# Batch 0's image tokens embedded alone, and a new order of a batch's steps

## Chip, cores and metric

The kernel runs on one core of a Trainium2 chip. The metric is device microseconds of one execution, as the median of several runs; lower is better.

## What is computed

All of it is float32. B = 8 sequences of L = 548 tokens of width D = 192: 36 image tokens, embedded from patches of 768 values, and 512 text tokens given as they are. Then one attention block (3 heads of 64, scores multiplied by a decay matrix before the softmax, a group norm over tokens and channels of each head) and one block of 16 experts, 8 of them weighted per token.

```python
h = concat([patches @ tok_w.T + tok_b, txt], axis=1)                  # (8, 548, 192)
x = layernorm(h)
q, k, v = x @ Wq.T, x @ Wk.T, x @ Wv.T                                # 3 heads of 64
s = (q @ k.T) / 8 * decay          # decay[l, m] = gamma_h ** (m - l) for m >= l, else 0
o = softmax(s) @ v
o = (o - mean) / sqrt(var + eps)   # mean and variance of a head over its tokens and channels
h = h + (o * gn_weight + gn_bias) @ Wo.T
x = layernorm(h)
p = softmax(x @ router_w.T); comb = the 8 largest of p, divided by their sum
h = h + sum over e of comb[:, e] * (gelu(x @ w1[e]) @ w2[e])          # widths 8 x 128, 8 x 256
```

## The kernel before

Five engines run their own instruction streams and meet at semaphores. The order on each engine is written out by hand; there is no planner. A product of float32 numbers is made of several passes over operands split into a rounded part (`_hi`) and a rest (`_lo`): ScalarE writes the rounded part (`copy`, L595), VectorE the rest (`sub`, L945).

**The prologue.** SP issues all loads in one queue (L310 to L321): `gammas`, the patches and the embedding weights in two halves each (`ld_pat`), the bias, the text of batch 0 (`ld_h0`), all attention weights in one transfer (`ld_aw`), the text of batches 1 to 7 (`ld_h`), a share of `w1`, `gn_w`, `gn_b`. Behind them in the same queue it stores the decay rows that VectorE has built (`decay_built`), waits until they have landed and loads them back shifted (`ld_decay`, L323 to L327). TensorE embeds the image tokens of all eight batches at once, 288 columns (L1279 to L1286); ScalarE adds the bias (`emb`, L601, L602), TensorE transposes them in sixteen products (L1291, L1292), VectorE copies them into `h` (`image_tokens`, L920). Before that VectorE has made `drow`, the powers of gamma by doubling (L882), and `aw_lo`, the rest of all attention weights (L890). Then the first layer norm and `x_transpose(0)`.

**A batch.** `body(b, tail, later, more, ahead)` exists once for each engine and is called for b = 0 to 7; `tail` is b > 0, `later` b > 1, `more` b < 7, `ahead` b < 6. In it the third head of batch b-1 is finished while batch b begins, and the output projection of batch b-2 is made inside batch b. TensorE's order is: `qk(b)` (three tiles: q01, q2 and k2, k01), third head's `probs_transpose(b-1, 2)`, `scores_pair(b)`, `attend(b-1, 2)`, `scores_third(b)`, `values(b)`, `project(b-2)`, `probs_transpose(b, 0)`, `attend(b, 0)`, `probs_transpose(b, 1)`, `x_transpose(b+1)`, `attend(b, 1)`, `gn_sums(b-1)`. VectorE's is: `qk_rest(b)` (four rests), `gn_stats(b-1, 0)`, `norm_stats(b+2)` (statistics of a layer norm two batches ahead), `apply_decay` of heads 0 and 1 (L982, with the negated maximum at L989), `normalise(b, 0)` (divides by the softmax's sum, L1006), `apply_decay(b, 2)`, `add_attention(b-2)` and `normalise(b, 1)`, `gn_partial(b-1)`, `x_ext(b+1)` (L954, sums that stand for the masked keys), `x_lo(b+1)`, `gn_variance(b-1)`, `normalise(b, 2)`. Of the third head, `normalise` does three of five tiles; ScalarE scales the other two in the next body:

```python
            def scale_probs(b):
                a.wait_ge(den_ready, nth(b, 1, 1))
                for I in range(2):
                    t = pr[0][:, OFF[I]:OFF[I] + WIDTH[I]]
                    last = a.activation(t, t, ACT.Copy, scale=inv_den[0][:, I:I + 1])
                last.then_inc(probs_scaled, 1)
```

ScalarE also rounds q and k (`qk_round`), makes the exponentials (`exps`, L674), copies transposed probabilities (`pt_copy`) and outputs (`o_copy`; the third head's output goes to both halves of the partitions, four copies), and rounds x (`x_hi`). GpSimd normalises the next batch (`norm_next`), takes the power -0.5 of variances (`rstd_of`, L454), splits a share of `w1` (`halve_w1`, L498 and L501, after `probs_ready` of the first head) and applies the group norm (`gn_coefficients`, `y_values`).

The eight banks of TensorE's accumulator are assigned to the steps by the tuples at L98 to L112; a step waits until what stood in its bank has been read.

**Batch 7 and the hand-over.** In batch 7 the first 512 tokens also get their second layer norm (`second_norm`), transposes (`x2_transpose`), `logits`, the routing (`router_shift`, `router_top`, `router_left`, `router_weights`) and `comb_transpose`; ScalarE copies the result to `ct`, SP stores it and loads it back as `gate`, one row spread over all partitions. The expert part is a loop over nine tiles of tokens and 24 steps (`up`, `gelu`, `weigh` with the gate, L1177, `act_round`, `act_rest`, `down`). In its first tile `beside_first(k)` finishes batch 7's third head and the projections of batches 6 and 7. The residual rows travel through `h_dram` (`store_h`).

Of the kernel before, what the change touches and what calls it, by code (L numbers as in the profile page):

```python
# [32 lines left out]
P = 128  # L33
B = 8
# [70 lines left out]
GN_BANK = 0  # L105
TILE_ORDER = (0, 1, 4, 2, 3)

LAST_PT1 = (1, 3, 0, 6)
LAST_PT2 = (4, 5, 4, 5)
LAST_WO = {5: (2, 7, 6), 6: (4, 5, 2), 7: (4, 5, 2)}  # L110
LAST_GN = {6: 5, 7: 3}
LAST_O = 2  # L112

ATTEND_TILES = ((0, 3, 4), (1, 2))
# [18 lines left out]
def early_fusion(nc, patches, txt, tok_w, tok_b, gammas, gn_w, gn_b, attn_w, w1, w2, out):  # L133
# [9 lines left out]
    with ctx:  # L143
# [102 lines left out]
        ld_aw, ld_pat, ld_gam, ld_gn = sem("ld_aw"), [sem("ld_pat0"), sem("ld_pat1")], sem("ld_gam"), sem("ld_gn")  # L246
# [12 lines left out]
        exp_done, den_ready, probs_ready = sem("exp_done"), sem("den_ready"), sem("probs_ready")  # L259
        probs_scaled = sem("probs_scaled")  # L260
# [40 lines left out]
        def _(sp):  # L301
# [54 lines left out]
            def body(b, tail, later, more, ahead):  # L356
# [11 lines left out]
                if later and more:  # L368
                    store_h(b - 2)
# [25 lines left out]
            store_h(LB - 2)  # L395
# [32 lines left out]
        def _(pool):  # L428
# [57 lines left out]
            def halve_w1(b):  # L486
# [33 lines left out]
            def y_values(t):  # L520
# [5 lines left out]
                for i in range(2):  # L526
                    pool.tensor_scalar(o[:, i, :], o[:, i, :], gscale[:, i:i + 1], gshift[:, i:i + 1], ALU.mult, ALU.add)
                pool.drain()
                for i, dst in enumerate((y01_hi, y2)):
                    pool.tensor_copy(dst[:, :], o[:, i, :]).then_inc(y_hi, 1)  # L530
                pool.drain()
                for i, (p0, lo, hi) in enumerate(((0, y01_lo, y01_hi), (HD, y2, y2))):
                    if i:
                        pool.drain()
                    pool.tensor_tensor(lo[p0:P, :], o[p0:P, i, :], hi[p0:P, :], ALU.subtract).then_inc(y_lo, 1)
# [21 lines left out]
            def body(b, tail, later, more, ahead):  # L557
# [33 lines left out]
        def _(sc_eng):  # L591
# [6 lines left out]
            a.wait_ge(ld_aw, 16)  # L598
            copy(aw_hi[:, :, :], aw_raw[:, :, :]).then_inc(aw_hi_ready, 1)
            a.wait_ge(emb_done, 1)  # L600
            a.activation(emb[:, 0, :], ps[:, 0, 0:B * IMG], ACT.Identity, bias=tokb[:, 0:1])  # L601
            a.activation(emb[0:HD, 1, :], ps[0:HD, 1, 0:B * IMG], ACT.Identity, bias=tokb[0:HD, 1:2]).then_inc(emb_copied, 1)  # L602

            def round_router():

                a.wait_ge(aw_lo_ready, 1)
# [30 lines left out]
            def scale_probs(b):  # L637

                a.wait_ge(den_ready, nth(b, 1, 1))
                for I in range(2):  # L640
                    t = pr[0][:, OFF[I]:OFF[I] + WIDTH[I]]
                    last = a.activation(t, t, ACT.Copy, scale=inv_den[0][:, I:I + 1])  # L642
# [1037 lines left out]
```

## Time and profile before

| | |
|---|---|
| median of 3 runs | 796.58 us (795.94 to 799.67) |
| profiled execution, its own time | 794.4 us |
| its span, first to last instruction | 792.1 us |
| TensorE busy, matmuls | 744.4 us (94%), 4400 instructions |
| VectorE busy | 551.0 us (70%) |
| ScalarE busy | 485.9 us (61%) |
| GpSimd busy | 155.8 us (20%) |
| transfers | 60.74 MB, mean 77 GB/s |

The span of the profile is what an order of instructions can change; the execution's own time lies 2.3 us above it. PE is TensorE, PEld its weight loads, DVE VectorE, ACT ScalarE, POOL GpSimd, SPq the queue from which SP issues transfers. A name such as L945 is a line of the kernel, often that of a helper: `sub` and `copy` serve many steps. "issue" is idle time for which the profile shows no wait.

### The profile page before, as it was taken

How to read it: one execution, taken by the hardware profiler on the slowest of the kernel's cores; microseconds unless marked ns; L12 is line 12 of the kernel's file. 1: busy time of each engine (PE TensorE's matmuls, PEld its weight loads, DVE VectorE, ACT ScalarE, POOL GpSimd, SP SyncE). 2: the span in 40 equal slices, each digit the busy share in tenths (PEclk: the TensorE clock that was granted, in tenths of full speed). 3: DMA queues.
4: the chain of work that ended last, by engine and by line, in shares of the span. 5: the costliest groups of instructions: out<-in, count | busy, mean ns of one | idle time of the engine just before them, and what ended most of it. 6: DMA issues, size and time to landing. Idle time of an engine off the chain costs nothing.

```text
span 792.1 us, 13238 instructions
## 1 busy us (share of the span) xinstructions
PE 744.4 (94%) x4400; PEld 635.0 (80%) x4400; DVE 551.0 (70%) x1548; ACT 485.9 (61%) x1087; POOL 155.8 (20%) x261
## 2 busy tenths in 40 slices
PE   6688898999988999999999999999999999999997
PEld 2577787888886777788888888888888888888885
DVE  5588888889788676576567566576666666665654
ACT  1368897897886846456556456556465564564443
POOL 2034436535542780010010010010000100100000
PEclk9689999999998999999999999999999999999999
DMA  7500010011031462242242241342241332412410
GB/s 223 167 2 21 21 42 22 23 42 43 2 100 41 121 184 60 77 127 72 58 115 69 77 128 39 86 125 55 78 120 52 86 104 62 109 62 70 113 50 19
DMA packets 44390, 60.74 MB, mean 77 GB/s; under 512 B 4018, under 2 KB 37762, under 8 KB 44322
## 3 DMA queue, kind: packets, MB, share of 16 engines
q1 hardware_dynamic: 44322, 59.91, 26.5%
q8 instruction: 34, 0.56, 0.3%
q14 instruction: 34, 0.28, 0.1%
HBM read 51.84 MB, written 8.05 MB: 76 GB/s over the span
## 4 chain that ended last, share of the span: by engine, by line
PE 71%; ACT 12%; DVE 7%; issue 4%; POOL 3%; DVEq 1%; POOLq 1%; DMA 0%; SPq 0%
PE ps L1271 67%; ACT pt L595 3%; ACT pr L674 3%; DVE sc L982 2%; ACT ot L595 2%; ACT pr L642 1%; ACT k_hi L595 1%; DVE pr L1006 1%; PE ps L1400 1%; POOL w_lo L553 1%; PE ps L1451 1%; DVE nm L989 1%; ACT xa_hi L595 1%; DVE k_lo L945 1%; POOLq L552 1%
## 5 line engine op out<-in xcount | busy, mean ns | idle before, releaser
L1177 DVE TENSOR_TENSOR act<-act,gate 128x480 f32<-128x480 f32 (+1 forms) x216 | 144.8, 671 | 115.8 <-ACT act L788 110.7
L1271 PE MATMUL ps<-x,w_hi 128*128 128x480 f32 (+1 forms) x648 | 217.0, 389 | 0.2 <-ACT act L788 0.2
L788 ACT ACTIVATE act<-ps 128x480 f32<-128x480 f32 (+1 forms) x216 | 123.7, 573 | 130.2 <-PE ps L1271 130.1
L1271 PE MATMUL ps<-x,w_lo 128*128 128x480 f32 (+1 forms) x432 | 165.9, 384 | 0.0
L945 DVE TENSOR_TENSOR act_lo<-act,act_hi 128x480 fp32r<-128x480 f32 (+1 forms) x216 | 145.0, 671 | 0.2
L1271 PEld LDWEIGHTS ps<-x,w_hi 128*128 128x128 f32 x648 | 121.6, 188 | 21.2 <-ACT act L788 0.7
L595 ACT ACTIVATE act_hi<-act 128x480 fp32r<-128x480 f32 (+1 forms) x216 | 130.7, 605 | 6.8 <-DVE act L1177 6.7
L1271 PEld LDWEIGHTS ps<-x,w_lo 128*128 128x128 f32 x432 | 81.2, 188 | 13.4
L1271 PE MATMUL ps<-act_hi,w_hi 128*128 128x480 f32 (+1 forms) x216 | 83.5, 387 | 4.5 <-DVE act_lo L945 4.5
L1271 PE MATMUL ps<-act_hi,w_lo 128*128 128x480 f32 (+1 forms) x216 | 82.5, 382 | 0.0
L1271 PE MATMUL ps<-act_lo,w_hi 128*128 128x480 f32 (+1 forms) x216 | 82.5, 382 | 0.0
L454 POOL TENSOR_TENSOR rstdb<-vepsb,neg_half 128x4 f32<-128x4 f32 x9 | 11.7, 1303 | 359.2 <-DVE vepsb L1069 359.2
L1271 PE MATMUL ps<-act_lo,w_r 128*128 128x480 f32 (+1 forms) x216 | 82.4, 381 | 0.0
L1271 PE MATMUL ps<-act_hi,w_r 128*128 128x480 f32 (+1 forms) x216 | 82.2, 381 | 0.0
L674 ACT ACTIVATE pr<-sc,nm 128x580 f32<-128x580 f32 (+4 forms) x120 | 66.4, 557 | 17.2 <-DVE nm L989 17.1
L1400 PE MATMUL ps<-ident,pr 128*128 128x128 f32 (+1 forms) x360 | 44.5, 274 | 16.9 <-ACT pr L642 6.9
L1400 PEld LDWEIGHTS ps<-ident,pr 128*128 128x128 f32 (+1 forms) x360 | 38.5, 132 | 22.0 <-issue 11.3
L595 ACT ACTIVATE pt<-ps 128x384 f32<-128x384 f32 (+3 forms) x120 | 46.2, 472 | 13.8 <-PE ps L1400 13.6
L982 DVE CUSTOM_DVE_ANT_0 sc<-ps,decay 128x548 f32<-128x548 f32 (+4 forms) x120 | 49.3, 453 | 4.7 <-PE ps L1271 4.5
L1271 PEld LDWEIGHTS ps<-act_hi,w_hi 128*128 128x128 f32 x216 | 40.4, 187 | 14.5 <-DVE act_lo L945 6.8
L1271 PEld LDWEIGHTS ps<-act_hi,w_r 128*128 128x128 f32 x216 | 40.5, 188 | 7.1
L1271 PEld LDWEIGHTS ps<-act_lo,w_r 128*128 128x128 f32 x216 | 40.5, 188 | 7.0
(181 smaller groups left out, 1257.0 us busy)
## 6 DMA issues: line engine op xcount, KB each, us to landing
gate<-comb_dram SPq DMA_DIRECT2D x112, 240.0 KB, 3.2
gate<-comb_dram SPq DMA_DIRECT2D x32, 256.0 KB, 3.8
w_raw<-w SPq DMA_DIRECT2D x16, 384.0 KB, 3.7
h_dram<-h SPq DMA_DIRECT2D x8, 384.0 KB
res<-h_dram SPq DMA_DIRECT2D x7, 360.0 KB, 4.4
out<-res SPq DMA_DIRECT2D x7, 360.0 KB, 3.2
h<-txt SPq DMA_DIRECT2D x3, 672.0 KB
decay_rows<-drow SPq DMA_DIRECT2D x1, 1014.0 KB, 8.4
```

The lines of the kernel that those rows point to most:

```text
L454: pool.tensor_tensor(rs[:, :], ve[:, :], neg_half[:, 0:n], ALU.pow)
L552: pool.drain()
L553: pool.tensor_tensor(w2_lo[:, part, :], raw[:, :, 0:P], w2_hi[:, part, :], ALU.subtract)
L595: return a.activation(dst, src, ACT.Copy)
L642: last = a.activation(t, t, ACT.Copy, scale=inv_den[0][:, I:I + 1])
L674: last = a.activation(pr[s][:r, cols], sc[s][:r, cols], ACT.Exp, bias=nm[s][:r, I:I + 1], accum_out=row_sum[s][:r, I:I + 1])
L788: a.activation(act[j % 3][:, 0:n], ps[:, up_bank(j), 0:n], ACT.Gelu_apprx_tanh).then_inc(gelu_done, 1)
L945: return dve.tensor_tensor(dst, src, hi, ALU.subtract)
L982: dve.tensor_tensor_reduce(out=sc[s][:r, OFF[I]:OFF[I] + n], in0=psf[:r, at:at + n], in1=decay[:r, hh, 0:n], scale=1.0 / 8, scalar=0.0 if ...
L1177: dve.tensor_tensor(act[j % 3][:, 0:n], act[j % 3][:, 0:n], gate[e % 4][:, 0:n], ALU.mult).then_inc(gated, 1)
L1271: return pe.matmul(dst, w, x, start=start, stop=stop)
L1400: return pe.transpose(ps[:n, bank, at:at + P], pr[s][:, src:src + n], ident[:, :])
```

## The change

It has four parts.

1. **Prologue.** The patches come as two inputs, batch 0's (36 columns) and the rest (252). SP loads batch 0's first, the rest only behind batch 0's text and the first part of the attention weights; the attention weights come in two transfers (q and k; all others). TensorE embeds batch 0 alone; the first 128 channels of the rest follow before `x_transpose(0)`, the last 64 inside batch 0 between the two heads' scores and the third's, and their transposes around `values(0)`. ScalarE's and VectorE's shares move likewise (`embedded`, `image_tokens(1)` to `(4)`, `weights_hi(i)`, `weights_lo(i)`). The powers of gamma are made in three portions with other steps between.
2. **Third head.** `scale_probs` is gone, and `normalise(b, 2)` scales all five tiles on VectorE. The third head's output is copied once (two copies), and `y2`, the group norm's statistics and values use 64 partitions for it.
3. **Order in a batch.** `qk` makes q01, k01, then q2 and k2; `scores_pair` waits for the first two tiles' rests alone. `o_copy(b-1, 1)` moves into the next body. `probs_transpose(b-1, 2)` waits for the first `q_lo` with all its groups. On VectorE, `norm_stats(b+2)` moves from before the first decay to after `add_attention(b-2)`, which is whole and after `normalise(b, 1)`. On GpSimd `halve_w1` goes ahead of `rstd_of(b+2)`. The banks are assigned anew.
4. **Batch 7.** `project(5)` and `add_attention(5)` stand where they do in other batches, `store_h(5)` is issued in SP's body, `x2_transpose` and `logits` move behind `attend(7, 0)`, and `up(0)`, `comb_transpose(0)`, `up(1)` end the batch. Small steps of `beside_first` change places.

The core of the diff:

```diff
-X_BANKS = (6, 1)
-QK_BANKS = (4, 6, 1)
-SCORE_BANKS = [(2, 4), (0, 5), (2, 6)]
-V_BANKS = ((4, NT - 1, 1), (0, 0, 2), (1, 2, 2))
-PT_BANKS = [(1, 3, 2, 6), (1, 3, 0, 4), (0, 3, 4, 5)]
-O_BANKS = (5, 3, 7)
-WO_BANKS = (5, 4, 0)
+X_BANKS = (1, 6)
+QK_BANKS = (4, 1, 6)
+SCORE_BANKS = [(0, 7), (3, 2), (0, 6)]
+V_BANKS = ((7, NT - 1, 1), (3, 0, 2), (4, 2, 2))
+PT_BANKS = [(4, 1, 0, 6), (6, 0, 3, 5), (3, 4, 5, 2)]
+O_BANKS = (4, 0, 5)
+WO_BANKS = (2, 3, 7)
...
 # SP
+            sp.dma_start(pat[:, :, 0:IMG], first_patches).then_inc(ld_pat[0], 16)
             for i in range(2):
                 part = slice(i * KT // 2, (i + 1) * KT // 2)
-                sp.dma_start(pat[:, part, :], patches[:, part, :]).then_inc(ld_pat[i], 16)
                 sp.dma_start(tokw[:, part, :], tok_w[:, part, :]).then_inc(ld_pat[i], 16)
             sp.dma_start(tokb[:, :], tok_b).then_inc(ld_pat[1], 16)
             load_h(0, 1, ld_h0)
-            sp.dma_start(aw_raw[:, :, :], attn_w).then_inc(ld_aw, 16)
+            sp.dma_start(aw_raw[:, :, 0:QK_W], attn_w[:, :, 0:QK_W]).then_inc(ld_aw[0], 16)
+            sp.dma_start(pat[:, :, IMG:B * IMG], patches).then_inc(ld_pat[2], 16)
+            sp.dma_start(aw_raw[:, :, QK_W:AW], attn_w[:, :, QK_W:AW]).then_inc(ld_aw[1], 16)
             load_h(1, B, ld_h)
...
 # GpSimd, body
+                halve_w1(b)
                 if ahead:
                     pool.drain()
                     rstd_of(b + 2, ln1_var, rstd, mv, veps, nmr, ln1_rstd)
-                halve_w1(b)
...
 # ScalarE, body
                 qk_round(b, 1)
                 if tail:
-                    scale_probs(t)
-                for part in (2, 3):
-                    qk_round(b, part)
+                    o_copy(t, 1, O_BANKS[1])
+                qk_round(b, 2)
+                qk_round(b, 3)
...
 # VectorE, normalise
-                for I in range(2 if hh == 2 else 0, NT):
+                for I in range(NT):
...
 # VectorE, body
                 qk_rest(b)
                 if tail:
                     gn_stats(t, 0)
-                if tail and ahead:
-                    dve.wait_ge(ln1_rstd, nth(b, 1, 2))
-                    norm_stats(b + 2, st6, mv, veps, ln1_var)
...
                 apply_decay(b, 0)
                 apply_decay(b, 1)
+                normalise(b, 0)
                 if not tail:
+                    dve.wait_ge(ld_h, 16 * NT)
+                    image_tokens(1)
+                    image_tokens(2)
+                    dve.drain()
                     norm_stats(1, st6, mv, veps, ln1_var)
-                normalise(b, 0)
                 apply_decay(b, 2)
-                if later and more:
-                    add_attention(b - 2, WO_BANKS, (0,))
...
+                normalise(b, 1)
+                if not tail:
+                    image_tokens(3)
+                    image_tokens(4)
+                    dve.drain()
+                if later:
+                    add_attention(b - 2, WO_BANKS)
+                if ahead:
+                    dve.wait_ge(ln1_rstd, nth(b, 1, 2))
+                    norm_stats(b + 2, st6, mv, veps, ln1_var)
...
 # TensorE
+            embed(0, 0, 0, IMG)
+            embed(1, 1, 0, IMG).then_inc(emb_done, 1)
             pe.wait_ge(emb_copied, 1)
             pe.wait_ge(consts, 2)
+            image_transpose(0)
+            pe.wait_ge(ld_pat[2], 16)
+            embed(0, 0, IMG, B * IMG).then_inc(emb_done, 1)
...
-                    probs_transpose(t, 2, (0,))
-                    pe.wait_ge(o_copied, nth(t, 3, 2))
                     pe.wait_ge(qk_lo, nth(b, 4, 1))
-                    probs_transpose(t, 2, (1, 2, 3))
+                    probs_transpose(t, 2, (0, 1, 2))
+                    pe.wait_ge(qk_lo, nth(b, 4, 2))
+                    probs_transpose(t, 2, (3,))
                 scores_pair(b, tail)
                 if tail:
                     attend(t, 2, O_BANKS[2])
+                else:
+                    embed(1, IMG_REST, IMG, B * IMG).then_inc(emb_done, 1)
                 scores_third(b)
...
                 attend(b, 0, O_BANKS[0])
+                if not more:
+                    pe.wait_ge(wo_added, nth(b - 2, 3, 3))
+                    x2_transpose(0, 1, LAST_X2[1])
...
+                if not more:
+                    up(0)
+                    comb_transpose(0, LAST_X2[1])
+                    up(1)
```

## Rows read from the trace of the kernel before

**Rows 1.** Busy time by stage: start:end, length, each engine's busy time (instructions).

```profile
0.00:29.10 29.10, 16.21 (x51) 7.29 (x51) 17.60 (x74) 5.75 (x8) 6.04 (x26) 0.88 0.76 234
...
29.10:300.00 270.90, 243.08 (x2007) 214.03 (x2008) 221.98 (x785) 210.85 (x581) 131.92 (x207) 0.96 0.18 54
```

**Rows 2.** Busy time by batch, the same columns, from one `x_ext` to the next.

```profile
112.66:140.88 28.22, 26.12 (x241) 23.63 (x240) 24.69 (x93) 23.83 (x69) 14.29 (x23) 1.00 0.10 30
...
197.36:225.37 28.01, 25.92 (x241) 23.61 (x240) 22.80 (x82) 23.93 (x69) 12.74 (x20) 1.00 0.09 31
```

**Rows 3.** Timeline, TensorE, batch 3: start, length, what, idle time before.

```profile
120.17 1.80 PE L1400 MATMUL ps<-ident,pr 128*68 128x128 f32 x15 [0.98 <-ACT pr L642]
...
122.41 0.50 PE L1271 MATMUL ps<-k_hi,q_hi 64*128 64x512 f32 x2 [0.44 <-ACT pt L595]
...
124.19 0.41 PE L1271 MATMUL ps<-k_hi,q_hi 64*128 64x292 f32 x2
```

**Rows 4.** Timeline, ScalarE, batch 3.

```profile
113.56 0.65 ACT L595 ACTIVATE xa_hi<-ps 128x580 fp32r<-128x580 f32 x1
...
118.70 1.33 ACT L642 ACTIVATE pr<-pr,inv_den 128x580 f32<-128x580 f32 x2
```

**Rows 5.** Timeline, VectorE, batch 3.

```profile
112.66 1.30 DVE L954 TENSOR_REDUCE ps<-ps 128x4 f32<-128x512 f32 x2
...
116.86 0.17 DVE L996 TENSOR_TENSOR den<-zero_score,lower_count 128x5 f32<-128x5 f32 x1
...
117.62 0.80 DVE L1006 TENSOR_SCALAR pr<-pr,inv_den 128x324 f32<-128x324 f32 x3
...
118.34 0.72 DVE L945 TENSOR_TENSOR q_lo<-ps,q_hi 128x548 fp32r<-128x548 f32 x1
...
122.81 1.37 DVE L900 BATCH_NORM_STATS2 st<-h 128x6 f32<-128x192 f32 x5
...
124.96 0.73 DVE L982 CUSTOM_DVE_ANT_0 sc<-ps,decay 128x548 f32<-128x548 f32 x1
...
130.71 1.58 DVE L1006 TENSOR_SCALAR pr<-pr,inv_den 128x580 f32<-128x580 f32 x5
...
132.21 0.71 DVE L982 CUSTOM_DVE_ANT_0 sc<-ps,decay 128x548 f32<-128x548 f32 x1
...
134.54 1.00 DVE L989 TENSOR_SCALAR nm<-mx 128x4 f32<-128x4 f32 x1
...
139.23 0.79 DVE L1012 BATCH_NORM_STATS2 gst<-ot 128x6 f32<-128x274 f32 x2
```

**Rows 6.** Timeline, GpSimd, batch 3.

```profile
133.54 1.97 POOL L501 TENSOR_TENSOR w_lo<-w_raw,w_hi 128x384 fp32r<-128x384 f32 x2
```

**Rows 7.** Timeline, prologue and batch 0: TensorE's first product, VectorE.

```profile
5.68 10.71 PE L1271 MATMUL ps<-pat,tokw 128*128 128x288 f32 x24 [5.68 <-DMA tokw<-tok_w]
...
22.45 1.47 DVE L920 COPY h<-ps 36x384 f32<-36x384 f32 x3
...
40.55 0.73 DVE L982 CUSTOM_DVE_ANT_0 sc<-ps,decay 128x548 f32<-128x548 f32 x1 [2.81 <-PE ps L1271]
```

**Rows 8.** SP's queue; transfers of the first 60 us: size, us to landing; queue's share.

```profile
23.26 0.55 SPq L324 DMA_DIRECT2D decay_rows<-drow  x1
...
decay_rows<-drow SPq DMA_DIRECT2D x1, 1014.0 KB, 8.4
...
decay<-decay_rows SPq DMA_DIRECT2D x1, 822.0 KB, 4.3
...
q1 hardware_dynamic: 6592, 7.70, 41.1%
```

**Rows 9.** Batch 7 to the first `weigh`: busy time, ScalarE's `ct`, VectorE.

```profile
225.37:268.24 42.87, 37.28 (x295) 32.13 (x294) 33.23 (x131) 34.29 (x95) 19.03 (x33) 0.92 0.24 70
...
261.32 0.59 ACT L595 ACTIVATE ct<-ps 16x512 f32<-16x512 f32 x1 [0.87 <-PE ps L1470]
...
268.24 1.29 DVE L1177 TENSOR_TENSOR act<-act,gate 128x512 f32<-128x512 f32 x2 [0.17 <-issue]
```

More of the change, by code:

```diff
@@ L130, in nth, with early_fusion @@
     return b * per + k
-def early_fusion(nc, patches, txt, tok_w, tok_b, gammas, gn_w, gn_b, attn_w, w1, w2, out):
+def early_fusion(nc, first_patches, patches, txt, tok_w, tok_b, gammas, gn_w, gn_b, attn_w, w1, w2, out):
     ctx = ExitStack()
@@ L525, in y_values @@
                 o = ot[t % 2]
[L526 to L535, printed above, removed]
+                for i, r in enumerate(Y_ROWS):
+                    pool.drain()
+                    pool.tensor_scalar(o[:r, i, :], o[:r, i, :], gscale[:r, i:i + 1], gshift[:r, i:i + 1], ALU.mult, ALU.add)
+                for i, hi in enumerate((y01_hi, y2)):
+                    pool.drain()
+                    pool.tensor_copy(hi[:Y_ROWS[i], :], o[:Y_ROWS[i], i, :]).then_inc(y_hi, 1)
+                for i, (lo, hi) in enumerate(((y01_lo, y01_hi), (y2[HD:P, :], y2))):
+                    pool.drain()
+                    pool.tensor_tensor(lo, o[:Y_ROWS[i], i, :], hi[:Y_ROWS[i], :], ALU.subtract).then_inc(y_lo, 1)
                 pool.drain()
@@ L635, in two @@
                 return ap.rearrange("p (a n) -> p a n", a=2)
[L637 to L642, printed above, removed]
-                last.then_inc(probs_scaled, 1)
             def qk_round(b, part):
-                dst, p0, i = ((q01_hi[:, :], 0, 0), (q2[0:HD, :], 0, 1), (k2_hi[HD:P, :], HD, 1), (k01_hi[:, :], 0, 2))[part]
+                dst, p0, i = ((q01_hi[:, :], 0, 0), (k01_hi[:, :], 0, 1), (q2[0:HD, :], 0, 2), (k2_hi[HD:P, :], HD, 2))[part]
                 a.wait_ge(qk_done, nth(b, 3, i + 1))
@@ L701, in o_copy @@
                 for half, n in enumerate(ATTEND_W):
-                    for p in ((0,), (HD,), (0, HD))[hh]:
-                        last = copy(ot[b % 2][p:p + HD, hh // 2, at:at + n], ps[HD * half:HD * half + HD, bank, 0:n])
+                    p = HD * (hh % 2)
+                    last = copy(ot[b % 2][p:p + HD, hh // 2, at:at + n], ps[HD * half:HD * half + HD, bank, 0:n])
                     at += n
@@ L756, in body @@
                 v_copy(b, (2,))
-                if not more:
-                    x2_round(0, 0, 5)
-                    x2_round(0, 1, 4)
                 exps(b, 1, (2, 3, 4))
@@ L931, in _ @@
             norm_join(st6, mv, veps, ln1_var)
-            for i in range(1, B // 2):
-                last = image_tokens(i)
-            last.then_inc(embt_copied, 1)
+            decay_powers(256, L - 1).then_inc(decay_built, 1)
             norm_share(0, rstd, nmr, ln1_rstd, xn, first_normed)
+            weights_lo(0)
             for t in (0, 1):
@@ L1164, in body @@
                 normalise(b, 2)
-                if not more:
-                    add_attention(b - 2, LAST_WO[b - 2])
             x_ext(0)
             x_lo(0)
+            weights_lo(1)
             iterations(body)
@@ L1316, in qk @@
                 for i in range(3):
-                    tile, bank = (0, 2, 1)[i], QK_BANKS[i]
+                    tile, bank = i, QK_BANKS[i]
+                    if i == 0 and not tail:
+                        pe.wait_ge(aw_lo_ready, 1)
                     if i == 0 and tail:
                         pe.wait_ge(o_copied, nth(b - 1, 3, 1))
+                        pe.wait_ge(pt_copied, nth(b - 1, 4 * H, 4 * 2))
                     ah, al, bh, bl = weights(tile * P, (tile + 1) * P)
@@ L1545, in down @@
+            x_transpose(0)
+            iterations(body)
             def down(j):
@@ L1661 @@
     arrays = {
[L1662 removed]
+        "first_patches": img.transpose(1, 0, 2)[:, :, 0:IMG],
+        "patches": img.transpose(1, 0, 2)[:, :, IMG:],
         "txt": f(txt),
```

326 lines of the change are left out of this document (174 added, 152 removed).

## The prediction

> **What bounds the kernel now.** I read the page first: TensorE is busy for 744.4 of 792.1 us, so all that an order of work can win lies in 47.7 us of its idle time, and a table by stage shows where. The prologue up to the first projection is 16.2 busy of 29.1 and leaves 12.9; the eight attention batches and the hand-over up to 300 us are 243.1 busy of 270.9 and leave 27.8 [rows 1]; so 7.0 of the 47.7 remain for the expert part's 492 us. The change leaves the expert part as it is after its first tile, so its gain must come from the first 300 us.
>
> One batch then, by the start of `x_ext` (L954) in each. Batches 1 to 6 take 27.4, 28.1, 28.2, 27.8, 28.7 and 28.0 us (batches 3 and 6 stand in [rows 2]), and 2 to 5 have a mean of 28.2, with TensorE busy about 26.1, VectorE 24.7 and ScalarE 23.8. In TensorE's timeline of batch 3 two gaps end on ScalarE: 0.98 us until it has scaled the third head (L642), 0.44 until it has copied `pt` [rows 3]; a third, before the second head's transposes, ends on VectorE. The 2.1 us idle are all that TensorE can be given back: 26.1 us is the floor of a batch. ScalarE's chain leads into the first: its scaling of two tiles takes 1.33 us and stands between the rounding of `q` and of `k` [rows 4]. VectorE has no long wait at all: its 24.7 us busy understate it, since each `drain` and each small operation leaves a little time that is neither busy nor free [rows 5]. That is the view which decides here.
>
> **The change in the steady batches.** Off ScalarE go the 1.33 us of scaling and two of the four copies of the third head's output. Onto VectorE goes the scaling: five tiles take 1.58 us where three take 0.80, so +0.78 [rows 5]. `norm_stats(b+2)`, 2.15 us from 122.81 to 124.96, today lies between `qk_rest` and the first decay, just while TensorE makes the scores VectorE needs. The change puts it behind `add_attention`, ahead of `gn_partial` and of `x_ext(b+1)`. There nothing covers it: behind it wait `x_ext`, then ScalarE's `x_hi`, then TensorE's next projections.
>
> So I add up VectorE's chain from one `x_ext` to the next, in the new order, with today's start-to-start times [rows 2, 4, 5]:
> - `x_ext` to `x_hi`: 0.65 and a handover, 0.73; both `x_hi` and the four remaining exponentials, 113.56 to 116.86: 3.30. Together 4.03. (VectorE's own `x_lo` and `gn_variance` are done at 3.9, and hide here.)
> - `normalise(b-1, 2)`: 116.86 to 118.34 is 1.48 with three tiles, +0.78 with five: 2.26.
> - `q_lo` of the first tile: 0.75, and 0.1 until TensorE sees it, since the third head's transposes now wait for it.
> - fifteen transposes: 1.80, less a little overlap, 1.73; their copies by ScalarE end as they do.
> - scores of tiles 0, 1 and 4: 122.41 to 124.19 plus the end of the last product, 2.04 [rows 3]. VectorE meanwhile has the other three parts of `qk_rest` and `gn_stats`, 2.9 us, and idles 1.0.
> - both decays and `normalise(b, 0)`, 124.96 to 132.21: 7.25.
> - third decay, `normalise(b, 1)` and `add_attention`, 132.21 to 139.23, less one drain: 6.93.
> - `norm_stats` 2.15 and `gn_partial`, 139.23 to 140.88, where batch 3 ends: 1.65.
>
> The sum is 28.9 us, where a batch now takes 28.2. The scaling leaves ScalarE's chain, but only to lengthen VectorE's, and the statistics lose their cover; TensorE waits for `q_lo` (1.0) and for `x_hi` (1.0) in place of the gaps it loses. TensorE's own chain in the new order ends about 0.9 before it is needed, so it does not decide. Batches 2 to 5: 4 x 0.7 = +2.8. Batch 1 has no `add_attention` (1.44): 27.5 against 27.4, +0.1. Batch 6 has no `norm_stats`: VectorE would need 26.75, TensorE brings `x_transpose` at about 27.0, so 27.0 against 28.0 [rows 2]: -1.0. Sum of the batches: +1.9.
>
> One term can go. In batch 3 a 128x4 negation (L989), elsewhere 0.17 us, takes 1.00 and ends at the same time as a subtraction of GpSimd (L501, 133.54 to 135.51) [rows 5, 6]. Six of the seven batches from 1 to 7 show 1.00, batch 4 shows 0.33. What starts the subtraction, `probs_ready` of the first head, is the same in the new order, so by the rows I keep the 0.85 us. If it went everywhere, a batch would be 28.05 and the sum of the batches -1.5. The Trainium skill has a rule for this (SBUF — State Buffer, section "SBUF: two separate sides"): VectorE in a two-port mode and GpSimd hold a shared pair of ports exclusively for a whole instruction, and the one that starts first makes the other wait. By that rule, the trace agrees, and a start moved by a fraction of a microsecond could turn the order round; that would be the 28.05.
>
> The bounds: a batch of 26.4 (TensorE's floor and a little) below, 29.4 above (0.5 more, should GpSimd's `y_values` also hold up the two new scalings). I take 28.9.
>
> **The prologue.** Today the first products start at 5.68 and take 10.71 us for 288 columns [rows 7]. With 36 columns an eighth of the streaming is left, and the weight loads between set the pace: 6 us, an estimate between an eighth and the whole of 10.7, nearer its middle. Then two transposes instead of sixteen, the copy of `aw_lo` out of VectorE's way, and the first layer norm's power at about 14.7 instead of 22.6: some 8 us earlier, as far as the first projection. The scores gain 1.4 more, since `k01` is now the second tile projected. They would be ready about 9 us earlier, and the decay could start at 32 instead of 40.55.
>
> But the decay matrix is not there. Its store is issued at 23.26, after all loads of SP's queue, and lands 8.4 later; its load follows and takes 4.3: it lands at 36.0 [rows 8]. Today that is hidden by 4.5 us. The store waits not for `decay_built` (about 16 after the change) but behind the loads, whose bytes stay the same. The packets become more: patches 256 to 1,536, attention weights 128 to 512, 1,664 in all. From nothing extra to, at the mean 60 ns of a packet (41.1% of 16 engines for 60 us by 6,592 packets [rows 8]), 6.2 us over 16 engines; since the bytes do not grow I take 0.8. The decay lands at 36.8 and VectorE starts at 36.9: 3.65 earlier than now [rows 7]. From 9 us, 5 are lost to this wait.
>
> Batch 0 then pays for what was moved into it. From the first decay to `x_ext(1)` it takes 16.65 us today (40.55 to 57.20). Added are four copies of image tokens (1.47 for three today [rows 7], so 1.9 with drains), ScalarE's second `emb` copy 0.5, ahead of the exponentials for which `normalise(0, 0)` waits, and 0.4 for the values, which now follow the image transposes: 19.5. `x_ext(1)` comes at 56.4, where it was 57.2: -0.8.
>
> **Batch 7 and the hand-over.** Projecting batch 5 earlier fills a gap of TensorE, but `x2_transpose(0, 1)` now waits for `add_attention(5)` (a bank of its own output), at 27.8 us after `x_ext(7)`; logits, shift, `second_norm(1)`, top and weights follow on VectorE, and `comb` is copied to `ct` at 37.6 after it. Today's copy ends at 261.91, 36.5 after it. The gates load from there: the first `weigh` starts 6.3 us behind it [rows 9]; I take 5.4 of that for the store and the gate, the rest for what VectorE still had to do: 43.0 after `x_ext(7)` against 42.87 now. The order inside is better, the end is set by the same road; VectorE no longer has the late `add_attention`, but waits for a gate instead. I take 0, from -3 (fewer waits in the first expert tile) to +3.5.
>
> **Sum.** -0.8 + 1.9 + 0 = +1.1 on the span of 792.1. That execution took 794.4, the median shown is 796.6, 2.2 above it; carried to the median: 797.6, rounded to 797.5. What this measurement can tell from no change is about 0.5%, 4 us.
>
> **The rivals.**
> 1. The batches fall to TensorE's floor. For it: TensorE is at 26.1 of 28.2 and two of its three gaps end on the removed scaling. Against: the chain above, which has no slack for it. Batches 1 to 6 at 26.4 each would save about 10: 787.
> 2. The decay comes sooner. The transfer engines are busy for 41.1% of the first 60 us [rows 8], so there is room; if the new order fills that, landing at 32 makes the prologue's 8 us real: -4.9 further, 792.
> 3. The other side: TensorE's clock at the hand-over. Batch 7 shows a mean granted clock of 0.92, the batches before it 1.00 [rows 2, 9]: 42.87 x 0.08 x 2, some 6.9 us at 0.5, the 1.2 GHz level. In the new order TensorE has nothing between `up(1)` at about 38 and the first `down` at 45 but two short pieces. If those gaps lower the clock as the first products of the expert part run, 6.8 us at half rate cost 3.4: 801. It decides once the gap before the first `down` exceeds some 2 us and the clock falls behind it and not before.
> 4. Nothing in the prologue is hidden and a batch costs 28.05: 795; inside no change.
>
> **Chances.** Forecast with rival 4: 0.56. Rival 1: 0.13. Rival 2, alone or with the stall gone: 0.12. Rival 3, or a batch of 29.4: 0.19. So faster 0.25, same 0.56, slower 0.19. Rival 1 in full and half of what lies above 801 stay outside: 790.5 to 801.5.
>
> **What the profile after would show.** The first decay starting right after `ld_decay`, near 37, with TensorE idle or embedding before it: right. A start near 32 makes rival 2 true. Batches of 28.5 to 29 with VectorE idle only before the first decay and TensorE waiting for `q_lo` and `xa_hi`: right; 26.5 makes it wrong. `norm_stats` between `add_attention` and `gn_partial` followed at once by `x_ext`: right. `ct` copied 37 to 38 after `x_ext(7)`: right; 34 would bring the end forward by 3.

## The result: half a per cent slower, and the profile after

The changed kernel takes 800.57 us (median of 12 runs, 797.01 to 802.74), the kernel before 796.24 (794.62 to 799.67): ratio 1.0052, 95% interval 1.0039 to 1.0066. That is +4.3 us where I had forecast about +1, inside the range. The two profiled executions stand further apart than the medians, 800.2 against 792.1 us of span, since the execution profiled of the kernel before (794.4) lies 1.8 below its median and that of the kernel after (802.0) 1.4 above. Of their 8.1 us this is the account, each term the difference of two starts in the traces: `x_ext(1)` comes 0.4 earlier (56.79 for 57.20); batches 1 to 6 take 4.6 more; `x_ext(7)` to the first `weigh` 0.3 more; from there to the end 3.6 more.

Busy time by stage of the kernel after (start:end, length, then PE, PEld, DVE, ACT, POOL with instructions, the granted clock, share and GB/s of the transfers), answering to [rows 1, 2, 9]:

```profile
0.00:36.15 36.15, 21.05 (x126) 17.07 (x126) 18.87 (x80) 9.79 (x18) 6.10 (x26) 0.96 0.73 214
36.15:56.79 20.64, 18.55 (x119) 15.12 (x121) 18.30 (x78) 12.80 (x40) 7.58 (x13) 0.73 0.01 2
113.15:142.29 29.14, 26.51 (x239) 23.69 (x239) 25.30 (x96) 21.88 (x64) 14.69 (x23) 1.00 0.10 29
142.29:172.55 30.26, 27.88 (x239) 25.19 (x239) 25.36 (x95) 21.89 (x64) 14.39 (x23) 0.94 0.09 29
201.40:229.60 28.20, 25.69 (x221) 23.73 (x221) 23.45 (x84) 21.50 (x63) 13.04 (x21) 0.94 0.07 23
229.60:272.80 43.20, 35.35 (x299) 30.35 (x297) 34.79 (x137) 31.20 (x88) 19.43 (x33) 1.00 0.25 72
272.80:800.20 527.40, 515.29 (x2486) 436.84 (x2486) 334.91 (x729) 286.31 (x530) 41.81 (x61) 0.99 0.30 85
```

ScalarE has lost 2 us a batch, as the change meant (21.9 where [rows 2] have 23.8), and the batch is longer. VectorE's busy time has grown by 0.6 (25.3 for 24.7), and its timeline has one long wait. VectorE's timeline of batch 3 after, the lines that answer to [rows 5]:

```profile
113.15 1.29 DVE L972 TENSOR_REDUCE ps<-ps 128x4 f32<-128x512 f32 x2
...
117.23 0.17 DVE L1014 TENSOR_TENSOR den<-zero_score,lower_count 128x5 f32<-128x5 f32 x1 [0.20 <-ACT pr L675]
...
118.29 1.58 DVE L1022 TENSOR_SCALAR pr<-pr,inv_den 128x580 f32<-128x580 f32 x5 [0.38 <-issue]
119.80 0.71 DVE L963 TENSOR_TENSOR q_lo<-ps,q_hi 128x548 fp32r<-128x548 f32 x1
...
124.60 0.73 DVE L1000 CUSTOM_DVE_ANT_0 sc<-ps,decay 128x548 f32<-128x548 f32 x1 [1.13 <-PE ps L1286]
...
131.86 0.72 DVE L1000 CUSTOM_DVE_ANT_0 sc<-ps,decay 128x548 f32<-128x548 f32 x1
...
134.19 1.02 DVE L1007 TENSOR_SCALAR nm<-mx 128x4 f32<-128x4 f32 x1
...
138.72 1.39 DVE L917 BATCH_NORM_STATS2 st<-h 128x6 f32<-128x192 f32 x5
...
140.78 0.77 DVE L1028 BATCH_NORM_STATS2 gst<-ot 64x6 f32<-64x274 f32 x2
...
142.29 0.69 DVE L972 TENSOR_REDUCE ps<-ps 128x4 f32<-128x512 f32 x1
```

The one wait on another engine's work of any length is the 1.13 us before the first decay. TensorE's timeline of the same batch shows its two long waits, for `x_hi` and for the first `q_lo`:

```profile
114.68 0.49 PE L1286 MATMUL ps<-xa_hi,aw_hi 128*128 128x274 f32 x2 [1.00 <-ACT xa_hi L597]
...
120.61 1.80 PE L1435 MATMUL ps<-ident,pr 128*68 128x128 f32 x15 [1.11 <-DVE q_lo L963]
122.44 0.50 PE L1286 MATMUL ps<-k_hi,q_hi 64*128 64x512 f32 x2
```

And GpSimd's subtraction, with whose end the negation L1007 ends (135.2):

```profile
133.21 1.98 POOL L504 TENSOR_TENSOR w_lo<-w_raw,w_hi 128x384 fp32r<-128x384 f32 x2
```

The prologue, by SP's queue, in place of [rows 8]: the text of batches 1 to 7 holds the queue for 11.5 us, and the decay matrix comes behind it.

```profile
8.16 11.53 SPq L309 DMA_DIRECT2D h<-txt  x3
...
23.98 0.43 SPq L328 DMA_DIRECT2D decay_rows<-drow  x1
31.60 0.38 SPq L331 DMA_DIRECT2D decay<-decay_rows  x1
```

VectorE's timeline shows what that costs, where [rows 7] had a wait of 2.81 for TensorE:

```profile
25.38 0.73 DVE L963 TENSOR_TENSOR k_lo<-ps,k_hi 64x548 fp32r<-64x548 f32 x1
36.15 0.73 DVE L1000 CUSTOM_DVE_ANT_0 sc<-ps,decay 128x548 f32<-128x548 f32 x1 [10.04 <-DMA decay<-decay_rows]
```

The hand-over in TensorE's timeline: short pieces between waits of 1.6, 2.2 and 2.7 us, and then the first `down` at the lower clock, a product every 0.43 us (277.77, 278.20) where experiment 7 has one every 0.23.

```profile
266.16 0.61 PE L1503 MATMUL ps<-ident,comb 128*16 128x128 f32 x4 [1.64 <-DVE comb L1131]
...
270.18 0.50 PE L1286 MATMUL ps<-x,w_hi 128*128 128x512 f32 x1 [2.24 <-ACT act L799]
...
275.15 1.17 PE L1435 MATMUL ps<-ident,pr 128*128 128x128 f32 x7 [2.67 <-ACT pt L597]
277.18 0.79 PE L1286 MATMUL ps<-act_hi,w_hi 128*128 128x512 f32 x1 [0.86 <-DVE act_lo L963]
277.77 0.63 PE L1286 MATMUL ps<-act_hi,w_lo 128*128 128x512 f32 x1
```

Last, stages cut where the granted clock changes, in batch 4 and at the hand-over:

```profile
142.70:146.10 3.40, 2.13 (x13) 1.67 (x14) 2.99 (x8) 3.09 (x10) 0.00 (x0) 1.00 0.00 0
146.10:149.50 3.40, 3.40 (x17) 3.40 (x17) 2.98 (x11) 1.92 (x6) 2.38 (x6) 0.50 0.01 2
...
270.00:275.80 5.80, 2.95 (x19) 2.42 (x20) 1.40 (x2) 2.19 (x6) 5.23 (x10) 1.00 0.78 230
275.80:282.60 6.80, 5.94 (x18) 3.84 (x17) 3.29 (x5) 2.76 (x6) 5.42 (x8) 0.50 0.53 138
```

At 0.50, 1.2 GHz, TensorE is busy for all of the 3.40 us in batch 4, but starts a projection's product every 0.23 us where 0.13 is usual. Batch 4 with such a stretch takes 30.26 us, its neighbours 29.14 and 28.85; there is another in batch 6 (204.1 to 207.5). The kernel before had none in batches 1 to 6. In all it had as much half-clock time as the changed one, 27.3 us ahead of the last products, but elsewhere: from 22.0 to 35.6, 39.0 to 45.9 and 250.7 to 257.5 (in batch 7), where the changed one has 33.5 to 47.1, the two stretches in batches and 275.8 to 282.6 (behind the first `weigh`).

### The profile page after: what moved, and what is told of

The parts are those of the page before. It is cut to its first block, busy times and chain, and to the rows that moved or that the text cites. A ratio compares the mean times of both kernels' runs of the same rounds, so it can differ in the third digit from the quotient of the medians.

```text
span 800.2 us, 13292 instructions
## 1 busy us (share of the span) xinstructions
PE 747.7 (93%) x4424; PEld 640.7 (80%) x4424; DVE 554.9 (69%) x1568; ACT 471.3 (59%) x1058; POOL 154.6 (19%) x261
## 4 chain that ended last, share of the span: by engine, by line
PE 68%; DVE 16%; ACT 4%; issue 3%; SPq 3%; DVEq 3%; DMA 2%; POOL 0%; POOLq 0%
PE ps L1286 64%; DVE sc L1000 4%; DVE pr L1022 3%; ACT pr L675 2%; DVE nm L1007 2%; SPq L309 2%; PE ps L1435 1%; DMA decay_rows<-drow 1%; PE ps L1484 1%; DVE h L1066 1%; DVE st L917 1%; DVEq L1005 1%; DMA gate<-comb_dram 1%; DVE act L1192 1%; ACT xa_hi L597 1%
## 5 line engine op out<-in xcount | busy, mean ns | idle before, releaser
L597 ACT ACTIVATE pt<-ps 128x384 f32<-128x384 f32 (+3 forms) x120 | 46.2, 470 | 12.1 <-PE ps L1435 11.5
```

The source lines that it names most:

```text
L597: return a.activation(dst, src, ACT.Copy)
```

## The experiments

Each is told as its difference from the changed kernel, unless it says otherwise. Ratios are to the kernel before.

**1. `norm_stats(b+2)` back before the first decay**, in batches 1 to 5.

```diff
                 if tail:
                     gn_stats(t, 0)
+                if tail and ahead:
+                    dve.wait_ge(ln1_rstd, nth(b, 1, 2))
+                    norm_stats(b + 2, st6, mv, veps, ln1_var)
...
-                if ahead:
+                if ahead and not tail:
```

> The changed kernel with one step put back: norm_stats(b+2) of batches 1 to 5 stands on VectorE before the first decay again, all else as changed. Theory (VectorE's chain has lost the cover of these statistics): the 1.0 us in which VectorE waits for the scores is filled, the first decay starts 1.1 us later and x_ext(b+1) comes 1.0 us earlier, so batches 1 to 5 take 27.9 us where they take 28.9, and TensorE's wait for x_hi (1.0 us) shrinks to some 0.1; 5 us less, 795 to 796 us. If the two short stretches of TensorE's lower clock in batches 4 and 6 came from these waits, they go too, and it is 793 to 795. Rival (the banks or the later q_lo set the batch): batches stay at 28.9, 800 us.

Measured: 796.74 us, ratio 0.9993 (0.9980 to 1.0007). Batches 2 to 5 take 28.45, 28.57, 28.26 and 28.27. The move is worth 0.5 us a batch, half of what I expected: 2.4 us of statistics go into a gap of 1.1 and push the first decay back by 1.4. In batch 3, L923, elsewhere 0.17 us, takes 0.61 and ends with a subtraction of GpSimd's `y_values` (124.73 to 126.08). This execution has no stretch at half clock in the batches, which accounts for 2.8 of the 4.9 us by which its profile is shorter than the changed kernel's; the median is 3.8 below.

**2. Scaling of two tiles back on ScalarE**, in `scale_probs` before `o_copy(b-1, 1)`, with its two semaphores.

```diff
-                for I in range(NT):
+                for I in range(2 if hh == 2 else 0, NT):
...
                 if tail:
+                    scale_probs(t)
                     o_copy(t, 1, O_BANKS[1])
```

> The changed kernel with ScalarE scaling two of the third head's five tiles again, between the rounding of k01 and o_copy(b-1, 1). Theory (one chain through both engines): VectorE is free 0.78 us earlier, but ScalarE, which now also has o_copy(b-1, 1) there, starts its copies of pt 1.3 us later, so the scores start at 10.0 us after x_ext in place of 8.9: a batch takes about 1 us more, 29.9, and the kernel 806 us. Rival (the scaling on VectorE is what made the batch long): 0.78 us less in each of six batches, 28.1, and 796 us.

Measured: 807.69 us, ratio 1.0145 (1.0128 to 1.0163). Batches 1 to 6 take 28.6 to 30.3; the first decay comes 12.5 us after `x_ext` where the change has 11.2. The rounding of q2 and k2 stands behind the scaling on ScalarE. This part of the change does pay, in the order around it.

**3. The decay matrix ahead of the text of batches 3 to 7** in SP's queue.

```diff
-            load_h(1, B, ld_h)
+            load_h(1, 3, ld_h)
...
             sp.dma_start(decay[:, :, :], shifted[:, :, 0:L]).then_inc(ld_decay, 16)
+            load_h(3, B, ld_h3)
...
                     dve.wait_ge(ln1_rstd, nth(b, 1, 2))
+                    if b == 1:
+                        dve.wait_ge(ld_h3, 16 * NT)
                     norm_stats(b + 2, st6, mv, veps, ln1_var)
```

> The changed kernel with SP's queue in another order: the text of batches 1 and 2, the share of w1 and gn_w, gn_b, then the decay rows' store and load, and the text of batches 3 to 7 last, with a wait for it before norm_stats(3). Theory (the decay matrix's way through the queue hides what the new prologue gained): the store is issued at about 14 to 16 us, the matrix has landed at 26 to 28 in place of 36.1, the first decay starts there and x_ext(1) comes at 47 to 49 where it comes at 56.8; 8 us less, 792 us. Rival (the transfers themselves are the limit, or the text of batches 1 and 2 comes too late): the first decay starts earlier, but x_ext(1) moves by less than 3 us.

Measured: 790.29 us, ratio 0.9931 (0.9914 to 0.9947): 10.3 below the changed kernel. SP's queue and VectorE's first decay:

```profile
8.38 1.99 SPq L309 DMA_DIRECT2D h<-txt  x3
...
14.08 0.38 SPq L328 DMA_DIRECT2D decay_rows<-drow  x1
22.00 0.38 SPq L331 DMA_DIRECT2D decay<-decay_rows  x1
```

```profile
26.84 0.73 DVE L1001 CUSTOM_DVE_ANT_0 sc<-ps,decay 128x548 f32<-128x548 f32 x1 [1.06 <-PE ps L1289]
```

The decay now waits for TensorE's scores, which are there at 26.8, 13.7 us earlier than in the kernel before. (In the changed kernel itself TensorE makes them from 24.15 to 27.1, and they wait there until 36.15.) So the prologue of the change was worth 13.7 us and all but 4.4 of it stood behind a transfer.

**4. The kernel before with `norm_stats(b+2)` behind `add_attention`**, that step of the change alone.

```diff
-                if tail and ahead:
-                    dve.wait_ge(ln1_rstd, nth(b, 1, 2))
-                    norm_stats(b + 2, st6, mv, veps, ln1_var)
...
+                if ahead:
+                    dve.wait_ge(ln1_rstd, nth(b, 1, 2))
+                    norm_stats(b + 2, st6, mv, veps, ln1_var)
```

> The kernel before with one part of the change alone: norm_stats(b+2) of batches 1 to 5 moves on VectorE from before the first decay to after add_attention(b-2), ahead of gn_partial. Theory (uncovered there): the first decay starts 0.5 us earlier, x_ext(b+1) about 1.6 us later, and with 0.2 us of slack in ScalarE's x_hi a batch takes 1.4 us more, 29.6 in place of 28.2; 7 us more, 803 us. Rival (ScalarE's chain sets the batch there, and VectorE has room): no more than 2 us, 796 to 798.

Measured: 798.71 us, ratio 1.0030 (1.0016 to 1.0044), batches 2 to 5 have a mean of 28.8 (28.2 before): 0.6 longer, not 1.4. VectorE's timeline of its batch 3 (the first decay, and the negation that took 1.00 in [rows 5]):

```profile
125.10 0.73 DVE L982 CUSTOM_DVE_ANT_0 sc<-ps,decay 128x548 f32<-128x548 f32 x1 [1.68 <-PE ps L1267]
...
134.51 0.17 DVE L989 TENSOR_SCALAR nm<-mx 128x4 f32<-128x4 f32 x1
```

The 2.15 us are uncovered, but GpSimd's `halve_w1`, which in the order of before stands behind `rstd_of` and so behind these statistics, starts only at 142.26: the stall of 0.85 goes, and the first decay comes 0.5 earlier. In the changed kernel `halve_w1` was moved ahead of `rstd_of`, and so the stall stayed.

**5. `halve_w1` after the second head's probabilities.**

```diff
-                pool.wait_ge(probs_ready, nth(b, H, 1))
+                pool.wait_ge(probs_ready, nth(b, H, 2))
```

> The changed kernel, in which GpSimd's halve_w1 starts after probs_ready of the second head instead of the first. Theory (VectorE's chain sets the batch, and 0.85 us of it is the negation L1007 that ends with GpSimd's subtraction): the negation falls from 1.02 to 0.17 us, batches 1 to 6 shorten by up to 0.85 each, to a mean of about 28.1 from 28.8; the span falls by 4 to 5 us to about 796. Rival: the subtraction then meets another small VectorE instruction, or delays GpSimd's power for the next statistics, and the batches stay at 28.8: 800.

Measured: 794.20 us, ratio 0.9965 (0.9952 to 0.9978): 6.4 below the changed kernel for one digit. Batches 2 to 5 take 28.00, 28.27, 27.99 and 28.00, and batch 6 26.53. Of the 6.9 us by which batches 1 to 6 are shorter in this profile, 2.8 are the two half-clock stretches, which it lacks, and 4.0 the stalls. VectorE's timeline of batch 5, in which the negation of the third head is back at 0.17:

```profile
180.51 0.73 DVE L1000 CUSTOM_DVE_ANT_0 sc<-ps,decay 128x548 f32<-128x548 f32 x1 [1.20 <-PE ps L1286]
...
190.03 0.17 DVE L1007 TENSOR_SCALAR nm<-mx 128x4 f32<-128x4 f32 x1
```

**6. Products that nobody reads in TensorE's two waits of a batch** (1 to 6); they change no output.

```diff
+                    filler(GN_BANK, 8)     # before the wait for q_lo
...
+                        filler(5, 7)       # after gn_sums
```

> The changed kernel, in which TensorE makes products that nobody reads in its two waits of about 1 us in batches 1 to 6: eight 128x128 transposes while it waits for the first q_lo, seven after gn_sums while it waits for x_hi. Theory (the granted clock of 0.5 at 146 to 150 us and at 204 to 208 us follows from those waits, and it is what makes batches 4 and 6 take 30.3 and 28.2 instead of 28.9 and 27.0): no stretch at 0.5 inside batches 1 to 6, batch 4 near 28.9, batch 6 near 27.5, the span 2 to 3 us less: 797.5. Rival: the falls come from something else (or the added products, some 0.1 us too long, cost as much as they save): batches of 28.9 to 29.2, falls remain somewhere, 800 to 802.

Measured: 798.11 us, ratio 1.0012 (0.9998 to 1.0026), 2.5 below the changed kernel. The profiled execution has no stretch at half clock in batches 1 to 6; batch 4 takes 28.83, batch 6 26.77.

**7. The same at the hand-over**: 12 and 16 products behind `up(0)` and `up(1)`, 18 between the groups of `pt`.

```diff
                     up(0)
+                    filler(2, 12)
                     comb_transpose(0, LAST_X2[1])
                     up(1)
+                    filler(2, 16)
...
                     probs_transpose(LB, 2, (0, 1), LAST_PT2)
+                    filler(2, 18)
```

> The changed kernel, in which TensorE makes 12, 16 and 18 products that nobody reads around comb_transpose and between the groups of pt in the first expert tile. Theory (the granted clock of 0.5 from 275.8 to 282.6 us follows from TensorE's waits of 1.6, 2.2 and 2.7 us before it, and takes about 3.4 us of the first expert tile): that stretch is gone or starts before the first weigh, and the time from the first weigh to the end falls by 3 us: span 797. Rival: the first expert tile is longer because of its order (the last groups of pt behind act_round), and only 0 to 1 us comes back: 800.

Measured: 798.39 us, ratio 1.0024 (1.0006 to 1.0042), 2.2 below the changed kernel. Its stage from the first `weigh` to the end, and the first `down` in TensorE's timeline:

```profile
270.58:794.80 524.22, 514.43 (x2502) 436.67 (x2500) 337.29 (x729) 286.53 (x530) 43.69 (x61) 1.00 0.30 86
```

```profile
274.23 0.50 PE L1286 MATMUL ps<-act_hi,w_hi 128*128 128x512 f32 x1 [0.30 <-DVE act_lo L963]
274.56 0.39 PE L1286 MATMUL ps<-act_hi,w_lo 128*128 128x512 f32 x1
```

524.2 against 527.4: 3.2 us come back, and the kernel before had 523.9. The batches of this kernel are those of the change, yet this execution had no stretch at half clock in them either: batch 4 took 28.83 and batch 6, in the first row here, 26.78. The second row is batch 6 of experiment 3, whose order there is the same, with a stretch (193.5 to 196.9):

```profile
200.65:227.43 26.78, 24.43 (x221) 22.30 (x221) 23.33 (x85) 21.38 (x63) 13.06 (x21) 1.00 0.08 25
```

```profile
190.54:218.78 28.24, 25.73 (x221) 23.81 (x221) 23.41 (x84) 21.50 (x63) 13.08 (x21) 0.94 0.07 23
```

So a stretch inside a batch costs 1.4 us, and whether one comes changes from one execution to the next. That this is part of why 12 runs of the change spread over 5.7 us is likely: those above 801 us have a mean granted clock of 0.981 to 0.984, those below 800 one of 0.984 to 0.988. In the medians the gain of this edit is not clear of the noise: its interval touches that of the change (1.0039 to 1.0066).

**8. Edits 1, 3 and 5 together.**

> The changed kernel with three edits together: norm_stats back before the first decay (alone: -4.9 us in the span), the decay matrix stored and loaded before the text of batches 3 to 7 (alone: -11.3), halve_w1 after the second head. Theory (the three act at different places of VectorE's chain, and add up; with the norm early, L1007's stall is again 0.85 in six batches, and going it leaves batches near 27.5): span 789 - 5 - 3 to 5 = 779 to 781, ratio near 0.98. Rival (TensorE, 26.1 us busy in a batch and waiting for x_hi, becomes the bound, or the clock falls oftener as it waits less evenly): 784 to 787.

Measured: 782.64 us, ratio 0.9824 (0.9799 to 0.9849), span 781.9, just outside what the theory gave, and better than the rival. Batches 4 and 5 take 27.97, no less than with edit 5 alone. VectorE and GpSimd at the end of its batch 4:

```profile
156.94 0.76 DVE L1038 TENSOR_TENSOR gtmp<-gmv 128x2 f32<-128x2 f32 x1
```

```profile
155.72 1.96 POOL L505 TENSOR_TENSOR w_lo<-w_raw,w_hi 128x384 fp32r<-128x384 f32 x2
```

The stall has moved: now a product of 128x2 numbers, elsewhere 0.16 us, waits for the end of the subtraction, at 157.7.

**9. Edits 3 and 5 without edit 1.**

> The changed kernel with the decay matrix ahead of the text of batches 3 to 7 and with halve_w1 after the second head, but norm_stats where the change put it (late). Theory (in the kernel with all three edits the early norm_stats gives nothing, since GpSimd's subtraction then meets VectorE's small subtraction L1038 in gn_partial, 0.76 us in place of 0.16): batches of 28.0 here too, ratio as with three edits, 0.982 within 0.002. Rival (the early norm_stats does give 0.5 us a batch): 785, ratio 0.986.

Measured: 783.53 us, ratio 0.9832 (0.9809 to 0.9855). The early `norm_stats` gives nothing once the other two are in: theory right.

**10. Experiment 8 with the subtraction of `halve_w1` behind the start of `x_ext(b+1)`**, and `rstd_of(b+2)` ahead of `halve_w1`.

```diff
+                if b < LB:
+                    pool.wait_ge(xt_ext, nth(b + 1, 2, 1))
                 for c in range(2):
                     last = pool.tensor_tensor(w1_lo[:, c, cols], w1_raw[:, c, :], w1_hi[:, c, cols], ALU.subtract)
```

> The changed kernel with norm_stats early, the decay matrix early, and halve_w1 in two pieces on GpSimd: the power of rstd_of(b+2) first, the rounding of w1 after the second head, its subtraction (1.96 us) only when x_ext(b+1) has started, where VectorE reads the accumulator. Theory (a small VectorE instruction on the SBUF that meets this subtraction waits for its end, and large ones that read the accumulator don't): L1038 takes 0.16 instead of 0.76, batches 2 to 5 take 27.4 instead of 28.0 to 28.4, the span is 3 us below the 781.9 of the three edits: 779. Rival: the power or the subtraction meets another instruction there (the negations in the decays, or x_lo), and the batches stay at 28.0 or above: 782 or more.

Measured: 783.78 us, ratio 0.9831 (0.9810 to 0.9851); batches 4 and 5 27.95. VectorE's timeline around the start of batch 4:

```profile
129.44 0.16 DVE L1043 TENSOR_TENSOR gtmp<-gmv 128x2 f32<-128x2 f32 x1
...
130.10 1.30 DVE L978 TENSOR_REDUCE ps<-ps 128x4 f32<-128x512 f32 x2 [0.26 <-PE ps L1351]
131.67 0.76 DVE L969 TENSOR_TENSOR xa_lo<-ps,xa_hi 128x580 fp32r<-128x580 f32 x1 [0.27 <-ACT xa_hi L603]
...
142.12 0.71 DVE L929 TENSOR_SCALAR veps<-mv 128x5 f32<-128x5 f32 x1
```

The stall is gone (0.16), and the batch is as long: `x_ext` now waits for TensorE's transposes, and L929, elsewhere 0.17 us, takes 0.71 and ends with a subtraction of `y_values`, so that stall has only changed its place. My theory was right about the stall and wrong about its worth.

**11. The same with the products of experiment 7.**

> As the run before with halve_w1 in two pieces, and with TensorE's added products around comb_transpose and between the groups of pt (12, 16 and 18). Theory (they keep the granted clock at 1.00 through the first expert tile, which gave 3.1 us from the first weigh to the end when they were added alone): 1 to 3 us below that run, 776 to 778. Rival (the clock's falls are elsewhere by now, before the first weigh): within 1 us of it.

Measured: 782.04 us, ratio 0.9813 (0.9790 to 0.9837). From the first `weigh` to the end 524.6 us, and 524.2 without the added products, where the half-clock stretch (253.5 to 256.9) began before the first `weigh` (255.7) and was over before the first `down` (259.3). The rival was right in substance; the batches are 27.96 again, and one (batch 1) has a stretch at half clock. Experiments 8 to 11 can't be told from each other; all are 1.7 to 1.9% faster than the kernel before.

## Why the prediction came out as it did

**The steady batch: right, by its own terms.** 28.9 forecast; batches 2, 3 and 5, which have no half-clock stretch, take 28.83, 29.14 and 28.85. By the lines of batch 3 above: 4.08 until the exponentials are done (4.03 forecast), 2.57 for the denominators and `normalise(b-1, 2)` (2.26; 0.38 of it is an idle time before the scalings for which the profile shows no wait, in batch 3 alone, and about what makes this batch 0.3 longer than 2 and 5), 0.81 for `q_lo` (0.85), 1.83 for the transposes (1.73), 2.16 for the scores with VectorE idle 1.13 (2.04; 1.0), 7.26 and 6.86 (7.25, 6.93), 2.06 for `norm_stats` (2.15), 1.51 for `gn_partial` (1.65). TensorE waits where I said, for `q_lo` 1.11 and for `x_hi` 1.00. Rival 1, TensorE's floor, is out: batches 3 and 5 stay 2.4 us or more above its busy time (26.5 of 29.14, 26.4 of 28.85).

**The stall of GpSimd: right that it stays, right what it is worth.** I gave 28.05 for a batch without it; experiment 5 has 28.0. The reason I gave, that its trigger is the same, holds only together with the new place of `halve_w1` (experiment 4: with the old one the stall goes by itself). The Trainium skill's rule (SBUF — State Buffer, section "SBUF: two separate sides"), that one of the two engines holds the shared ports for a whole instruction, fits what is seen: three different small instructions (1.02, 0.61, 0.76 us in place of 0.17) each ended within 0.03 us of a GpSimd subtraction that had begun before them. Not every small instruction did so: the 128x1 negation at 125.43 in batch 3 kept its 0.15 us with half a microsecond of such a subtraction still to go.

**The cost of the move of `norm_stats`: too high when taken alone.** As a term of VectorE's sum it was right, but undone it gives back 0.5 a batch, not 1, and made alone in the old order it costs 0.6, not 1.4. The sum of one engine's chain tells the price of a step in one order; in another order something else waits.

**The prologue: the wait right, its size wrong, and hidden.** I had the scores about 9 us earlier, at 32; experiment 3 shows 26.8, 13.7 earlier. Two sizes were off. The embedding of 36 columns took 4.2 us (5.02 to 9.22) where I had 6. And I gave the granted clock no term: before, the transposes of x and the first projections fell into the stretch at 0.50 from 22.0 to 35.6 and took 2.4 and 7.3 us; in the new order they are over before the clock falls at 33.5, and take 1.25 and 4.8, 3.5 us less together. I had the decay matrix 0.8 late through 1,664 more packets, at 36.8; there were 1,680 more (8,272 for 6,592 in the first 45 us), and the store was issued 0.7 later than before (23.98 for 23.26) and landed in 7.6 us instead of 8.4, so that the matrix was there at 36.0, as before. The first decay at 36.15 thus was forecast within 0.8 (36.9), while VectorE idled 10.0 us where I had 5. The store stands behind the loads of SP's queue and not behind `decay_built`: right. Rival 2 did not happen in the change, and is what experiment 3 makes of it, larger than I gave it: 790, not 792.

**Batch 0: 20.6 where I had 19.5.** The copies of image tokens were right: 1.6 and 0.34 us for 1.9. Missing were 0.65 in one instruction L923 (0.82 at 56.06, where 0.17 is usual), which again ends with a GpSimd subtraction (54.89 to 56.85), and TensorE at a mean clock of 0.73: with the same stall but the clock at 1.00 it takes 20.1 (experiment 8: 26.49 to 46.55).

**The batches' sum: +1.9 forecast, +4.6 in the profile.** With batch 4 at 28.83 and batch 6 at 26.78, as in experiment 7, the sum would be +1.8. The other 2.8 are the two half-clock stretches: the mechanism of rival 3, in a place where I had not looked for it. TensorE's waits of a batch stood far apart before (in batch 3 at 120, 122 and 138 us); now three of 0.21, 1.00 and 0.27 stand within its first 3 us, and both stretches begin within 1 us of the third. That these waits bring the falls about is likely (filled, they were gone, and the median fell by 2.5) but not shown: one execution with the waits unfilled had none either. Two other orders had a stretch at another place of batch 1, likewise behind waits close together: 0.77 and 1.40 us in experiment 2 (fall at 69.1), 0.74 and 0.82 in experiment 11 (67.3).

**The hand-over: rival 3 was right, and I took 0.** `ct` is copied 37.8 us after `x_ext(7)` (37.6 forecast), the first `weigh` starts 43.2 after it (43.0). But from the first `weigh` to the end it takes 3.6 us more, which are lost in the first expert tile. The fall that stood in batch 7 before cost nothing that shows there (batch 7 at a clock of 1.00 is no shorter, 43.2 for 42.9); behind the first `weigh` it does. I had priced rival 3 at 3.4 and set it to decide above some 2 us of wait before the first `down`: the waits were 2.2 and 2.7, and in the profile of experiment 7, where they are filled, 3.2 us come back. I gave this case 0.19 together with a longer batch; the 2 us of wait in my own list of steps spoke for more.

**The total: inside the range, with luck.** In the two profiles the difference is 8.1 us where my terms gave 1.1. Of the 7.0 between them, 3.6 lie behind the first `weigh`, which I took as 0 (3.2 of them the clock, by experiment 7), 2.7 the batches, nearly all half-clock stretches, and 0.7 the prologue and batch 7. The prologue's part looks better than it was: the decay came 0.8 earlier than forecast and batch 0 took 1.1 longer, and the two nearly cancel. In the medians, +4.3 stays 0.9 below the upper end of the range, which rival 3 had set. So the steady batch was forecast by its mechanism; the total was held by the width of the range.

## What to carry to other kernels

Before you shorten a stretch, ask of each input that its end needs when it will be there: 9 of 14 us won by a shorter prologue stood behind one transfer issued last in a queue, and moving it brought 10. When a step leaves one engine's chain, add up the chain it joins in the new order, drains and handovers included; that sum came within 0.3 us. Give TensorE's clock a term of its own wherever an order moves its waits. A tiny instruction that takes five times its usual time and ends with one on GpSimd is a price worth removing by moving the other engine's start, but look what it meets next.

## What the runs showed of the hardware

- VectorE products and scalings of 128x2 to 128x5 numbers that take 0.16 to 0.17 us took 0.61, 0.71, 0.76, 0.82 or 1.02 when a GpSimd subtraction of 1.4 to 2 us was under way. Beside one, the 128x1 negation kept its 0.15 us and BATCH_NORM_AGGREGATE on 128x2 (55.20 in batch 0) its 0.18; decays and `x_lo`, which read the accumulator, kept their times (0.73, 0.76).
- Beside GpSimd's power (1.17 us) a product of 128x5 numbers was held up by no more than 0.05 us: 0.21 at 136.92 in experiment 1, with over 1.1 us of the power to go.
- TensorE's clock fell to 0.50 for 3.4 us in the middle of batches in which it was never idle for more than 1.2 us at a time, in some executions and not in others of the same order; each cost 1.4 us. The prologue's first projections took 7.3 us at 0.50 for most of their time, 4.8 at 1.00.
- Products that nobody reads, 46 of them in 5.5 us at the hand-over, left the profile 3.2 us shorter from the first `weigh` to the end, with no stretch at half clock there; the median was 2.2 lower, which is within the noise.
- With 1,680 more packets for the same 7.70 MB in the first 45 us, the decay's store was issued 0.7 us later and landed 0.8 us faster.
